# GpSimd computes no powers between the blocks of four transfers of its scatters

## The chip, the cores and the metric

One of the eight cores of a Trainium2 chip runs the whole kernel, in one launch. The metric is the time of one execution on the device, in microseconds (us). A time given for the kernel is the median of several executions.

## What is computed

The layer is a "macaron": feed-forward, attention, feed-forward, over 4096 tokens of 256 numbers.

```python
x = x + 0.5 * ffn(layernorm(x))
x = x + attn(layernorm(x))
x = x + 0.5 * ffn(layernorm(x))

def ffn(x):                                 # both times with the same weights
    tidx, tw = route(x)                     # 4 of 16 experts per token, and their weights
    routed = sum(tw[k] * mlp(x, expert[tidx[k]]) for k in range(4))
    return routed + mlp(x, shared)          # the shared expert is 2 x 128 wide
```

Each `mlp` is `silu(x @ gate.T) * (x @ up.T) @ down.T` with 128 inner channels for an expert. The attention stage is a state-space scan with a convolution and a gate; the change does not touch it. All of it is in fp32.

## The kernel before

**Tokens and blocks.** The 4096 tokens lie in SBUF as 32 blocks of 128 (`xn`, `xin`). They are routed in three groups g = 0, 1, 2 of 12, 12 and 8 blocks. Two neighbouring blocks or tiles form a pair, the unit of TensorE's work.

**Scatter.** Once VectorE has worked out where each token's four copies go (`rows`, line 719), GpSimd writes every block of `xn` four times to a table `xg` in HBM, sorted by expert: four indirect DMAs of 128 rows of 1 KB each (function `scatter`, line 426). A group's scatter starts when its `rows` are ready, and the groups come one after another. Before some blocks GpSimd computes a power of one element per partition into a tile `idle` that nobody reads (function `rest`, line 419). `REST_SCATTER` (line 38) says before which: 2 in group 0 (before blocks 2, 4, 6, 8 and 10), 1 in groups 1 and 2 (before every block but the first). During the scatter of group 0 GpSimd also computes the inverse standard deviations of the last four tiles of tokens, a power with a purpose (`rstd_of`, line 413): behind blocks 0 to 3 in the first stage, behind blocks 1, 2, 4 and 6 in the second.

**Experts.** SyncE loads four blocks of sorted rows at a time from `xg` into `xq` (line 335), the first ones when group 0 is scattered, the later ones when their group is. TensorE works through 78 pairs of sorted tiles. For each pair it turns the rows (`turn_x`, line 993, 4 matmul records), multiplies them by gate and up (`gate_up`, line 1025, 8 records), multiplies an earlier pair by down (`down`, line 1054, 4) and turns `h` of the pair before (`turn_h`, line 1038, 2): 18 matmul records in all. ScalarE copies the turned rows (`f_xT`, line 490), computes silu (line 503) and takes the output (`f_yo`, line 513); VectorE multiplies (line 768) and copies `h` turned (line 776). SyncE stores the output to `yg` (line 339).

**Order.** A written list of events sets what all engines do: while group 0 is being scattered, TensorE is on the router's products (line 1009) and the shared expert (lines 1030 and 1054); while group 1 is, on the last of these and the first pairs of group 0; while group 2 is, on further pairs of group 0. VectorE routes the next group meanwhile.

**Gather.** When enough pairs are stored, GpSimd fetches for each block four times 128 rows of `yg` into one of four buffers `gbuf` (function `gather_group`, line 452), and VectorE adds them up (line 791). A gather has no power between its blocks (`REST_GATHER` is zero); its first four blocks go out back to back, and later ones wait for VectorE to free a buffer.

Everything here happens in both feed-forward stages, the first at about 0 to 560 us, the second at about 1120 us to the end, apart from small differences in the order of the events.

Of the kernel before, what the change touches and what calls it, by code (L numbers as in the profile page):

```python
# [34 lines left out]
XQ = 4  # L35
YO = 4
GBUF = 4
REST_SCATTER = (2, 1, 1)
REST_GATHER = (0, 0, 0)
PIECES_W = [(0, SH), (SH, SH + 6), (SH + 6, SH + 11), (SH + 11, NU)]  # L40
FIRST_NORMALIZE = {("route", 5): 3, ("both", 6): 4, ("both", 8): 5, ("shared", 2): 6, ("shared", 3): 7}
# [101 lines left out]
def ffn_stage(nc, whole, consts, label, base, banks, src, dst, scratch, w, shared_sems, nth, spots=None):  # L143
# [250 lines left out]
    def gpsimd(pool, other):  # L394
# [22 lines left out]
        def rest():  # L417

            G.tensor_tensor(idle[:, rests[0]:rests[0] + 1], ones_m[:, 0:1], half_neg[:, 0:1], ALU.pow)
            rests[0] += 1  # L420

        def scatter(g, b):
            if REST_SCATTER[g] and b and b % REST_SCATTER[g] == 0:
                rest()
            for k in range(4):
                G.indirect_dma_start(xg[0:USED[g] * P, :], bass.IndirectOffsetOnAxis(ap=rows[g][:, b, k:k + 1], axis=0),  # L426
                                     xn[:, SUB * TILE0[g] + b, :], None, bounds_check=USED[g] * P - 1,
                                     oob_is_err=False).then_inc(scattered[g], 16)
# [1942 lines left out]
```

## Time and profile before

| | |
|---|---|
| median of three executions | 1679.23 us (1678.22 to 1689.73) |
| the profiled execution | 1694.23 us |
| its span, first to last instruction | 1692.4 us |
| its mean granted TensorE clock | 0.899 |
| GpSimd busy | 951.7 us (56%) |
| indirect DMAs of the scatters | 256 |
| indirect DMAs of the gathers | 256 |
| powers of line 419 | 46 |

The profiled execution's own time lies 1.83 us above its span. In the rows, PE is TensorE's matmuls, PEld its weight loads, DVE VectorE, ACT ScalarE, POOL GpSimd and SPq the queue of SyncE. Starts are counted from the first instruction. The ends of matmuls are modelled, so a matmul can have been finished later than its record says; a few per cent of the matmul records can be missing. "issue" is a wait for nothing that the profile shows, "remote" one that nothing in the profile of this core explains. An indirect DMA's record on POOL is the time in which GpSimd makes its descriptors, not the transfer.

### The profile page before, as it was taken

Reading aid. Unit: us, or ns where it says so; the run is one execution under the profiler, and the core shown is the slowest. Engines: PE = TensorE matmul, PEld = TensorE weight load, DVE = VectorE, ACT = ScalarE, POOL = GpSimd, SP = SyncE. Lnnn points to the kernel's source line nnn. Section 1 sums busy time; section 2 is a strip of 40 time slices with the busy share of each in tenths; the row PEclk is TensorE's granted clock in tenths of the full one; section 3 lists DMA queues with packets and bytes.
Section 4 is the critical chain, followed back from the end, with each engine's and each line's share of the span. In section 5 each row is a group of like instructions: output and inputs, shape, how many; then the busy total and the mean of one; then the engine's idle time right before and its main releaser. Section 6 shows DMA issues by size and latency. Waiting matters only on the chain.

```text
span 1692.4 us, 22687 instructions
## 1 busy us (share of the span) xinstructions
PE 1345.6 (80%) x6904; PEld 1143.0 (68%) x6904; DVE 905.1 (53%) x2190; ACT 658.4 (39%) x1088; POOL 951.7 (56%) x1002
## 2 busy tenths in 40 slices
PE   5847577968959969999999999969564599696890
PEld 5736465857847747888888887857554488585780
DVE  5626251224436798888888878765353122352453
ACT  2222232423424445656656665523311134242330
POOL 2664835054264668878878977417466701634535
PEclk9869788989989979999999999989687899798895
DMA  9951344546555520001000000234324435565633
GB/s 362 401 185 66 112 144 143 168 154 200 191 182 182 185 89 13 26 15 38 26 26 25 25 23 11 87 131 168 113 103 140 149 118 171 164 212 187 196 131 99
DMA packets 86917, 218.39 MB, mean 129 GB/s; under 512 B 16272, under 2 KB 28560, under 8 KB 85904
## 3 DMA queue, kind: packets, MB, share of 16 engines
q1 hardware_dynamic: 62224, 149.82, 25.1%
q0 software_dynamic: 24576, 67.14, 12.5%
q8 instruction: 58, 0.95, 0.2%
q14 instruction: 59, 0.48, 0.1%
HBM read 109.43 MB, written 107.48 MB: 128 GB/s over the span
## 4 chain that ended last, share of the span: by engine, by line
PE 54%; DVE 16%; issue 15%; another core or an unknown queue 9%; ACT 3%; POOL 2%; DVEq 0%; POOLq 0%; DMA 0%; ACTq 0%
PE ps L1025 14%; PE ps L1054 9%; PE ps L993 5%; PE ps L1030 5%; DVE at_xs L1784 3%; PE ps L1984 3%; PE ps L1986 3%; PE ps L1985 3%; PE ps L2045 2%; PE ps L1038 2%; DVE f_xin L791 2%; PE ps L1009 2%; PE ps L2046 1%; PE ps L2034 1%
## 5 line engine op out<-in xcount | busy, mean ns | idle before, releaser
L452 POOL DMA_INDIRECT f_gbuf<-yg,f_rows x256 | 263.0, 1027 | 389.8 <-DMA yg<-f_yo 243.7
L426 POOL DMA_INDIRECT xg<-f_xn,f_rows x256 | 253.8, 991 | 180.1 <-DVE f_rows L719 110.0
L1025 PE MATMUL ps<-f_wgu,f_xT 128*128 x1248 | 322.9, 405 | 17.9 <-issue 15.2
L1054 PE MATMUL ps<-f_wd,f_hT 128*128 x624 | 181.2, 417 | 144.2 <-issue 81.9
L1025 PEld LDWEIGHTS ps<-f_wgu,f_xT 128*128 128x128 f32 x1248 | 244.9, 207 | 53.1 <-issue 22.1
L768 DVE TENSOR_TENSOR f_h<-ps,f_sg 128x256 f32<-128x256 f32 x156 | 66.1, 424 | 377.8 <-ACT f_sg L503 242.1
L1054 PEld LDWEIGHTS ps<-f_wd,f_hT 128*128 128x128 f32 x624 | 124.3, 205 | 175.9 <-issue 159.1
L490 ACT COPY f_xT<-ps 128x512 f32<-128x512 f32 x212 | 124.2, 586 | 219.6 <-remote 100.0
L503 ACT ACTIVATE f_sg<-ps 128x256 f32<-128x256 f32 x156 | 60.1, 385 | 289.6 <-PE ps L1025 160.9
L1030 PE MATMUL ps<-f_xT,f_wgu_sh 128*128 128x256 f32 x512 | 135.2, 422 | 24.7 <-issue 12.0
L1784 DVE SCALAR_TENSOR_TENSOR at_xs<-at_raw,at_taps,at_xs 128x512 f32<-128x512 f32 x136 | 138.4, 1020 | 6.9 <-POOL at_xs L1435 4.2
L513 ACT COPY f_yo<-ps 128x512 f32<-128x512 f32 x156 | 91.5, 587 | 120.9 <-PE ps L1054 55.2
L1030 PEld LDWEIGHTS ps<-f_xT,f_wgu_sh 128*128 128x128 f32 x512 | 107.0, 215 | 43.7 <-issue 24.6
L791 DVE SCALAR_TENSOR_TENSOR f_xin<-f_gbuf,f_w,f_xin 128x256 f32<-128x256 f32 x256 | 128.3, 502 | 12.4 <-DMA f_gbuf<-yg,f_rows 5.4
L993 PE MATMUL ps<-ident,f_xq 128*128 128x128 f32 x624 | 105.9, 298 | 16.4 <-DVE f_counts L652 10.1
L776 DVE COPY f_hT<-ps 128x256 f32<-128x256 f32 x156 | 66.0, 423 | 95.9 <-remote 64.8
L2045 PE MATMUL ps<-at_wout,at_ynT_hi 128*128 128x256 f32 x512 | 98.0, 292 | 6.6 <-DVE at_ynT_lo L1793 5.2
L1434 POOL TENSOR_SCALAR at_tap<-at_raw,at_taps 128x512 f32<-128x512 f32 x56 | 93.2, 1665 | 5.6
L993 PEld LDWEIGHTS ps<-ident,f_xq 128*128 128x128 f32 x624 | 83.2, 155 | 18.5 <-issue 17.7
L2045 PEld LDWEIGHTS ps<-at_wout,at_ynT_hi 128*128 128x128 f32 x512 | 81.1, 195 | 12.7 <-DVE at_ynT_lo L1793 8.2
L1477 POOL TENSOR_TENSOR at_S_split<-at_S,at_S_split 64x1024 fp32r<-64x1024 f32 x31 | 74.2, 2394 | 10.5 <-ACT at_S_split L1670 10.3
L1435 POOL TENSOR_TENSOR at_xs<-at_xs,at_tap 128x512 f32<-128x512 f32 x56 | 75.8, 1354 | 4.7
(258 smaller groups left out, 2655.7 us busy)
## 6 DMA issues: line engine op xcount, KB each, us to landing
f_xq<-xg SPq DMA_DIRECT2D x78, 512.0 KB
yg<-f_yo SPq DMA_DIRECT2D x156, 256.0 KB
xg<-f_gbuf SPq DMA_DIRECT2D x39, 512.0 KB, 5.9
f_wgu<-in_gate_up SPq DMA_DIRECT2D x4, 1280.0 KB
f_xin<-in_x SPq DMA_DIRECT2D x8, 512.0 KB, 7.0
xg<-f_xn,f_rows POOLq DMA_INDIRECT x256
f_gbuf<-yg,f_rows POOLq DMA_INDIRECT x256
x<-f_xin SPq DMA_DIRECT2D x8, 512.0 KB, 4.1
```

The source lines that it names most:

```text
L426: G.indirect_dma_start(xg[0:USED[g] * P, :], bass.IndirectOffsetOnAxis(ap=rows[g][:, b, k:k + 1], axis=0), xn[:, SUB * TILE0[g] + b, :], N ...
L452: G.indirect_dma_start(gbuf[:, n % GBUF, k, :], None, yg[0:USED[g] * P, :], bass.IndirectOffsetOnAxis(ap=rows[g][:, b, k:k + 1], axis=0), ...
L490: A.copy(xT[:, k % 2], turned(k)).then_inc(xT_ready, 1)
L513: A.copy(yo[:, n % YO, :], y_ps[:, yy % 2]).then_inc(y_out, 1)
L791: ins = V.scalar_tensor_tensor(out=xin[:, n // SUB, n % SUB, :], in0=gbuf[:, n % GBUF, k, :], scalar=w4[g][:, b, k:k + 1], in1=xin[:, n // ...
L993: last = T.transpose(turned(k)[:, c:c + P], of[s][:, d * P:(d + 1) * P], ident[:])
L1025: last = T.matmul(gu_ps[:, j % 2, s * 2 * P:(s + 1) * 2 * P], x_of(k, s, d), weight(wgu[:, :, d, :], experts[s]), start=(d == 0), stop=(d ...
L1030: last = T.matmul(gu_ps[:, j % 2, half * 2 * P:(half + 1) * 2 * P], wgu_sh[:, experts[0], d, half * P:(half + 1) * P], xT[:, k % 2, 2 * d ...
L1054: last = T.matmul(y_ps[:, yy % 2, s * D:(s + 1) * D], hT[:, i % 4, s * P:(s + 1) * P], weight(wd if kind == "routed" else wd_sh, experts[i ...
L1434: link(G.tensor_scalar(tap0[:], raw[:, j % 2, 0:TILE], taps[:, j, 0:1], None, ALU.mult))
L1784: ins = V.scalar_tensor_tensor(out=acc, in0=raw[:, j % 2, k:k + TILE], scalar=taps[:, j, k:k + 1], in1=acc, op0=ALU.mult, op1=ALU.add)
L2045: nc.tensor.matmul(xu_ps[:, 0, 0:D], ynT_hi[:, j, :], wout[:, j, i, :], start=(j == 0 and i == 0), stop=False)
```

## The change

The constant that places the powers of the scatters is set to zero, so that `rest` is never called. Nothing else changes.

```diff
-REST_SCATTER = (2, 1, 1)
+REST_SCATTER = (0, 0, 0)
```

On POOL, group 0's scatter in the first feed-forward stage (`f_rows_150` holds the addresses of group 0, L413 are the inverse standard deviations; the piece begins behind block 2 of 0 to 11):

```order
 L413 TENSOR_TENSOR f_rstd<-f_var,f_half_neg 128x4
-L419 TENSOR_TENSOR f_idle<-ones,f_half_neg 128x1
-L426 DMA xg<-f_xn,f_rows_150 8192x256 x8
-L419 TENSOR_TENSOR f_idle<-ones,f_half_neg 128x1
-L426 DMA xg<-f_xn,f_rows_150 8192x256 x8
-L419 TENSOR_TENSOR f_idle<-ones,f_half_neg 128x1
-L426 DMA xg<-f_xn,f_rows_150 8192x256 x8
-L419 TENSOR_TENSOR f_idle<-ones,f_half_neg 128x1
-L426 DMA xg<-f_xn,f_rows_150 8192x256 x8
+L426 DMA xg<-f_xn,f_rows_150 8192x256 x32
 L1441 TENSOR_SCALAR at_rate<-at_rate 128x1
```

Four runs of eight DMAs become one run of 32.

On POOL, the end of group 2's scatter in the first stage and, in the rows with a plus, what stands for the whole scatters of groups 1 (`f_rows_151`) and 2 (`f_rows_152`):

```order
-L426 DMA xg<-f_xn,f_rows_152 19968x256 x4
-L419 TENSOR_TENSOR f_idle<-ones,f_half_neg 128x1
-L426 DMA xg<-f_xn,f_rows_152 19968x256 x4
+L426 DMA xg<-f_xn,f_rows_151 14336x256 x48
+L426 DMA xg<-f_xn,f_rows_152 19968x256 x32
 L452 DMA f_gbuf<-yg,f_rows_150 128x256 x48
```

Runs of four become one run of 48 and one of 32. Between these two, POOL still waits for group 2's rows.

On POOL, group 0's scatter in the second stage (`f_rows_272`), behind block 2:

```order
-L426 DMA xg<-f_xn,f_rows_272 8192x256 x4
-L419 TENSOR_TENSOR f_idle<-ones,f_half_neg 128x1
-L426 DMA xg<-f_xn,f_rows_272 8192x256 x4
-L413 TENSOR_TENSOR f_rstd<-f_var,f_half_neg 128x4
-L426 DMA xg<-f_xn,f_rows_272 8192x256 x4
-L419 TENSOR_TENSOR f_idle<-ones,f_half_neg 128x1
-L426 DMA xg<-f_xn,f_rows_272 8192x256 x4
-L413 TENSOR_TENSOR f_rstd<-f_var,f_half_neg 128x4
-L426 DMA xg<-f_xn,f_rows_272 8192x256 x4
-L419 TENSOR_TENSOR f_idle<-ones,f_half_neg 128x1
```

Here a power stood between any two of the blocks 1 to 8; what is left are runs of eight between the powers of line 413, and one run of 20 behind the last of them. The order on all other engines is the same, row for row.

## Rows read from the trace of the kernel before

**Rows 1.** The page: busy time, and the chain that ended last, by engine

```profile
PE 1345.6 (80%) x6904; PEld 1143.0 (68%) x6904; DVE 905.1 (53%) x2190; ACT 658.4 (39%) x1088; POOL 951.7 (56%) x1002
PE 54%; DVE 16%; issue 15%; another core or an unknown queue 9%; ACT 3%; POOL 2%; DVEq 0%; POOLq 0%; DMA 0%; ACTq 0%
```

**Rows 2.** Line 419 over the whole span: duration ns min/median/max

```profile
L419 POOL TENSOR_TENSOR f_idle<-ones,f_half_neg x46: 527/592/697, 62.7 to 1349.2; 128x1 f32<-128x1 f32 x46
```

**Rows 3.** Timeline of POOL, scatter of group 0, first stage: start, duration, idle before

```profile
85.57 0.97 POOL L426 DMA_INDIRECT xg<-f_xn,f_rows  x1 [0.31 <-issue]
86.85 0.97 POOL L426 DMA_INDIRECT xg<-f_xn,f_rows  x1 [0.30 <-issue]
87.83 0.58 POOL L419 TENSOR_TENSOR f_idle<-ones,f_half_neg 128x1 f32<-128x1 f32 x1
...
89.95 1.13 POOL L426 DMA_INDIRECT xg<-f_xn,f_rows  x1 [0.30 <-issue]
```

**Rows 4.** Timeline of POOL and SyncE's queue: who waits for a scatter's end

```profile
236.13 0.97 POOL L426 DMA_INDIRECT xg<-f_xn,f_rows  x1 [23.42 <-DVE f_rows L719]
348.48 1.05 POOL L452 DMA_INDIRECT f_gbuf<-yg,f_rows  x1 [68.03 <-DMA yg<-f_yo]
121.92 1.74 SPq L335 DMA_DIRECT2D f_xq<-xg  x4
```

**Rows 5.** Timeline of ACT and PE in group 1's scatter, first stage

```profile
185.75 0.60 PE L993 MATMUL ps<-ident,f_xq 128*128 128x128 f32 x4
194.38 0.59 ACT L490 COPY f_xT<-ps 128x512 f32<-128x512 f32 x1 [5.38 <-remote]
200.10 0.38 ACT L503 ACTIVATE f_sg<-ps 128x256 f32<-128x256 f32 x1 [5.13 <-PE ps L1025]
211.61 0.38 ACT L503 ACTIVATE f_sg<-ps 128x256 f32<-128x256 f32 x1 [5.87 <-remote]
```

**Rows 6.** Timeline of ACT in a gather of the first stage, without powers

```profile
355.71 0.59 ACT L513 COPY f_yo<-ps 128x512 f32<-128x512 f32 x1 [2.29 <-remote]
465.12 0.39 ACT L503 ACTIVATE f_sg<-ps 128x256 f32<-128x256 f32 x1 [3.04 <-remote]
482.20 0.39 ACT L503 ACTIVATE f_sg<-ps 128x256 f32<-128x256 f32 x1 [10.03 <-remote]
```

**Rows 7.** Windows: stretch, length, PE, PEld, DVE, ACT, POOL busy (count), clock, DMA share, GB/s

```profile
145.00:160.00 15.00, 14.19 (x57) 11.72 (x58) 8.20 (x28) 2.12 (x5) 11.96 (x13) 0.81 0.26 89
160.00:213.00 53.00, 28.13 (x111) 22.90 (x109) 13.61 (x44) 11.17 (x21) 42.45 (x47) 0.77 0.31 107
1232.00:1253.00 21.00, 16.88 (x74) 14.08 (x75) 15.03 (x57) 3.50 (x7) 16.41 (x18) 0.84 0.36 123
1253.00:1298.00 45.00, 19.34 (x66) 14.70 (x64) 5.70 (x34) 5.05 (x10) 36.12 (x41) 0.73 0.36 122
236.00:281.00 45.00, 28.67 (x110) 22.27 (x110) 9.99 (x34) 7.78 (x15) 35.61 (x39) 0.81 0.43 145
1311.00:1355.00 44.00, 24.46 (x105) 19.70 (x104) 9.02 (x30) 7.40 (x14) 35.18 (x39) 0.85 0.42 148
300.00:345.00 45.00, 45.00 (x251) 40.03 (x250) 11.89 (x28) 21.40 (x42) 0.00 (x0) 1.00 0.50 164
1150.00:1184.00 34.00, 30.70 (x166) 26.73 (x167) 18.20 (x56) 11.34 (x25) 23.75 (x26) 1.00 0.31 117
1184.00:1211.00 27.00, 12.92 (x78) 11.14 (x76) 10.23 (x54) 9.73 (x17) 20.59 (x22) 0.77 0.28 97
86.00:121.00 35.00, 15.15 (x56) 12.04 (x56) 5.38 (x18) 7.01 (x11) 27.14 (x29) 0.64 0.46 164
```

**Rows 8.** Windows as in rows 7: three gathers without powers, POOL back to back

```profile
356.00:380.00 24.00, 8.66 (x33) 6.42 (x32) 5.08 (x11) 2.44 (x5) 18.17 (x19) 0.70 0.46 143
466.00:484.00 18.00, 4.20 (x20) 2.86 (x19) 2.69 (x6) 1.56 (x3) 13.83 (x14) 0.84 0.52 162
1545.00:1571.00 26.00, 9.24 (x38) 6.83 (x37) 5.00 (x11) 2.73 (x5) 19.05 (x20) 0.79 0.46 141
```

## The prediction

> **What bounds the kernel now.** I read the page first. TensorE is busy for 80% of the span and carries 54% of the chain that ended last; GpSimd is busy for 56% and carries 2% [rows 1]. So GpSimd's time is not what the kernel waits for, and a shorter GpSimd program gains nothing by itself. The next view is the line of the powers: 46 of them, 592 ns each, 27 us of GpSimd's time [rows 2]. The timeline of GpSimd then shows what one costs in place: between the starts of the DMAs at 86.85 and 89.95 lie 3.10 us with a power, where two steps without one take 2 x 1.28 us (85.57 to 86.85) [rows 3]. That is 0.54 us; I use 0.55.
>
> Who waits for a scatter's end? Group 2's scatter starts when VectorE has its rows, after 23.42 us of idle time behind group 1's. The first gather starts after 68.03 us of idle time behind group 2's. SyncE loads the first sorted rows at 121.92, right behind group 0's scatter, but TensorE multiplies the first of them only at 178 us [rows 4]. Nobody stands and waits for the last scatter of a group.
>
> The last view is the one that matters, the windows by stretch [rows 7]. With GpSimd silent (300 to 345 us) TensorE issues 251 matmul records in 45 us, 5.6 per us. In the scatters it issues far fewer: 111 in 53 us, 66 in 45, 56 in 35. The timeline says how this looks: TensorE turned rows at 185.75, and ScalarE, idle, copies them only at 194.38, with a wait that the profile puts to "remote"; two silus are 11.5 us apart (200.10 to 211.61) [rows 5], where a pair of 18 records would take 18/5.6 = 3.2 us. So TensorE's results arrive late while GpSimd issues indirect DMAs, and TensorE, the bound, stands still for want of them. This is where the change acts.
>
> **Does a pause of GpSimd help TensorE?** Three things say so. First, stretches of the second stage: from 1150 to 1184 a power stands between any two blocks (some of them the longer ones of line 413, and one wait), and TensorE issues 166 records in 34 us, 4.9 per us; from 1184 to 1211 a power stands only after each second block, and it issues 78 in 27 us, 2.9 per us [rows 7]. Second, the start of a group: in group 1 the pace holds for some 15 us (57 records, 3.8 per us) and 21 us (74 records), and breaks down after that [rows 7]. In the gathers, which have no powers, the first late result comes soon: ScalarE was free for it at 355.71 - 2.29 = 353.4 and started at 355.7, which is 4.9 to 7.2 us behind the first DMA at 348.48; I use 5.4 [rows 4, 6]. Third, the level it falls to: in three gathers 33, 20 and 38 records in 24, 18 and 26 us, together 91/68 = 1.34 per us, with silus 17.1 us apart in the second [rows 6, 8]. With powers the scatters show 111/53 and 66/45, together 177/98 = 1.81 per us [rows 7].
>
> **The rule that speaks against this.** The rows show TensorE slowed while GpSimd issues indirect DMAs (rows 7, 66 records in 45 us against 251). The Trainium skill, "SBUF — State Buffer", section "Who interferes with whom", says that only the ports shared by VectorE and GpSimd cause contention and that TensorE has its own. By that rule the powers cost TensorE nothing and protect it from nothing, and the sum would be zero. The trace agrees that a DMA's record is not stretched, but TensorE's results do come late, so the rule is not the whole story here.
>
> **The change part by part.** Removed are 46 powers: 5 + 11 + 7 in each of two stages. Nothing is added; no DMA moves past another or past a wait. POOL's queue behind them (the next group's wait, the gathers) only comes earlier. For each scatter I count what TensorE gets done in it before and after. A scatter gets shorter by 0.55 us for each power. In it TensorE keeps its first pace for 5.4 us, then runs at S records per us, and what is left is done at 5.6 per us. S is the unknown: no scatter without powers is in the trace. Its nearest rows are the gathers without powers, so I take S = 1.35. Its ends are 1.81 (pauses do not matter to the level) and 1.0. The lower one is an estimate: a scatter's DMAs follow each other without the longer pauses that in [rows 7] go with 1.81, and the step from 1.81 to 1.34 is carried on by three quarters.
>
> - Group 1, first stage: 168 records in 68 us. After: 62 us, with 5.4 x 3.8 = 21 and 56.6 x 1.35 = 76, so 71 are left, 12.7 us. Sum 74.7, that is +6.7 us.
> - Group 1, second stage: 140 records in 66 us. After: 60 us, with 5.4 x 3.5 = 19 and 54.6 x 1.35 = 74; 47 left, 8.4 us: +2.4.
> - Group 2, first stage: 110 records in 45 us. After: 41.2 us, with 5.4 x 3.8 = 21 and 35.8 x 1.35 = 48; 41 left, 7.3 us: +3.5.
> - Group 2, second stage: 105 records in 44 us. After: 40.2 us, 21 and 47; 37 left, 6.6 us: +2.8.
> - Group 0, second stage: 244 records in 61 us. Four powers go, 58.8 us are left. The runs are now of eight with the power of line 413 between them, then one of 20. If the runs of eight hide as they did, only the last 20 us are slow: 20 x 1.35 + 38.8 x 4.9 = 217, 27 left, 4.8 us: +2.6. If the second half of each run of eight is slow too, 30 us are: 40 + 141, 63 left, 11.2 us: +9.0. I take the middle, +6.
> - Group 0, first stage, from 86 to 121: already slow, 56 records in 35 us. After: 33.4 us with 45; 11 left, 2 us: +0.4; the stretch before 86 loses one power, no change.
>
> The sum is 6.7 + 2.4 + 3.5 + 2.8 + 6 + 0.4 = 21.8, say +22 us. All these stretches lie one behind the other on TensorE, which sets the end, so they add. The gathers keep their order and cost nothing. With S = 1.0 the slow 240 us of these six (57 + 55 + 36 + 35 + 25 + 33) lose 240 x 0.35 / 5.6 = 15 us more, +37. With S = 1.81 they gain 240 x 0.46 / 5.6 = 20 us, which makes +2: the pause then helps only through the later onset.
>
> The profiled execution took 1694.23 us, 15 us above the median of the runs shown. Its time would become 1716; carried to the median of 1679.23 the forecast is 1701 us, with a range of its own of 1681 (S = 1.81) to 1716 (S = 1.0).
>
> **The rivals.**
>
> *A fixed share per DMA (faster).* Each indirect DMA might let a fixed number of TensorE's results through, pause or not. Then a power in a slow stretch only delays all, and its removal gives its full 0.55 us. 33 of the 46 powers lie in slow stretches (3, 9 and 5 in the groups of the first stage; 2, 8 and 6 in the second): 33 x 0.55 = 18 us, 1661 us. For it: ScalarE's steps of 5.7 us (194.38 to 200.10) [rows 5] look like four DMAs and their power. Against it: gathers without powers let fewer records through per DMA, 91/53 = 1.7 [rows 8] against 177/71 = 2.5 in group 1's scatters (88 operations of POOL less 17 powers) [rows 7], and the pace of 4.9 from 1150 to 1184. It decides if the records per DMA stay at 2.5.
>
> *The powers touch nothing.* The late results come with the scatter and would come as late without powers; the level differs in gathers for their own reasons (they write SBUF, scatters write HBM). What is saved on GpSimd is saved where nobody waits: 1679 us. This is also what the rule on the ports gives. For it: GpSimd's 2% of the chain. Against it: the difference between 4.9 and 2.9 records per us within one scatter.
>
> *Choked (slower still).* Without any pause TensorE's results might not get through at all behind the first 5.4 us: S = 0, and 240 x 1.35 / 5.6 = 58 us on top of the 22: 1759 us. Against it: the gathers still let 1.34 through [rows 8].
>
> **How the numbers follow.** The forecast has 0.60, the fixed share 0.13, no effect 0.20, choked 0.07. Run to run, about 1%, 17 us, can be told from no change. Of the forecast's 0.60, which spans 1681 to 1716, 0.50 lies above 1696, 0.08 within 1% and 0.02 below. Slower: 0.50 + 0.07 + 0.01 of the second rival = 0.58. Same: 0.08 + 0.17 + 0.02 of the first = 0.27. Faster: 0.11 + 0.02 + 0.02 = 0.15. The range runs from 1666, which leaves out most of the fixed share, to 1726, beyond S = 1.0 by another 10 us for a lower clock behind longer stalls: the clock was 0.64 to 0.85 in slow stretches and 1.00 in the free one [rows 7].
>
> **What would show it.** In the new profile: no row of line 419; POOL 46 x 0.55 = 25 us shorter in all its scatters; the first late result of ScalarE 5 to 6 us behind the start of groups 1 and 2, not 15 to 20; silus in group 1 some 13 to 18 us apart, not 11.5; 1.0 to 1.8 records per us in the slow part. It is wrong if group 1's scatter of 62 us holds 2 or more records per us of TensorE, or if the pairs done by its end are as many as before. It is half wrong if the level falls and the kernel is no slower, because something that I count as TensorE's work waits for VectorE anyway.

## The result, and the profile after

The changed kernel takes 1752.68 us (median of four executions, 1750.12 to 1754.06), the kernel before, run beside it, 1684.48 us (1678.22 to 1694.87). The ratio is 1.0453, with a 95% interval of 1.0401 to 1.0506: slower by 68 us. The forecast was 1701 us, with a range up to 1726. Here and below the ratio is estimated from undisturbed executions, so it need not be the quotient of the medians (1.0405 here); five executions of the experiments were left out of it as disturbed, among them three of the 26 of the kernel before on the first chip, A (1674.85, 1883.65 and 4528.40 us).

The profiled execution took 1754.06 us, its span is 1752.2 us against 1692.4. The page of the changed kernel, busy times and the chain that ended last, as [rows 1]:

```profile
PE 1340.0 (76%) x6904; PEld 1138.9 (65%) x6904; DVE 904.8 (52%) x2190; ACT 658.3 (38%) x1088; POOL 927.4 (53%) x956
PE 51%; issue 17%; DVE 16%; another core or an unknown queue 9%; ACT 3%; POOL 2%; DMA 1%; DVEq 0%; POOLq 0%; SPq 0%; ACTq 0%
```

GpSimd has 46 operations and 24.3 us less, as it should. No engine has more work; 60 us were added, and TensorE was busy in none of them (1340.0 us against 1345.6). The timeline of GpSimd shows where, in the starts of the scatters and gathers (as [rows 4]; start, duration, operation, idle time before it):

```profile
260.16 0.98 POOL L426 DMA_INDIRECT xg<-f_xn,f_rows  x1 [47.32 <-DVE f_rows L719]
...
381.27 1.05 POOL L452 DMA_INDIRECT f_gbuf<-yg,f_rows  x1 [80.31 <-DMA yg<-f_yo]
...
1270.58 0.97 POOL L426 DMA_INDIRECT xg<-f_xn,f_rows  x1 [25.95 <-DVE f_rows L719]
...
1360.32 0.97 POOL L426 DMA_INDIRECT xg<-f_xn,f_rows  x1 [28.50 <-DVE f_rows L719]
...
1492.14 1.06 POOL L452 DMA_INDIRECT f_gbuf<-yg,f_rows  x1 [91.12 <-DMA yg<-f_yo]
```

In the first stage, group 2's scatter starts at 260.16, before at 236.13, and the first gather at 381.27, before at 348.48 [rows 4]. GpSimd's wait for VectorE's rows ahead of group 2 doubled, from 23.42 to 47.32 us. Taken from start to start, so that each stretch is a scatter and the work behind it, the loss lies here:

| stretch, from a scatter's start to the next one's or the gather's | stage 1 | stage 2 |
|---|---|---|
| group 0 | +6.0 us | +3.6 us |
| group 1 | +18.0 us | +11.8 us |
| group 2 | +8.8 us | +9.9 us |

The six sum to 58.1 of the 59.8 us that the span grew by. The rest of the kernel, attention above all, lost 1.7 us.

The windows of the changed kernel (length, then busy time and records of PE, PEld, DVE, ACT, POOL, granted clock, DMA share, GB/s) answer [rows 7]:

```profile
151.00:167.00 16.00, 14.45 (x63) 12.02 (x64) 7.85 (x27) 1.74 (x4) 12.10 (x13) 0.90 0.27 92
167.00:213.00 46.00, 8.46 (x24) 5.80 (x22) 3.16 (x8) 0.97 (x2) 35.17 (x36) 0.58 0.30 103
213.00:260.00 47.00, 34.86 (x174) 30.13 (x174) 24.57 (x116) 19.82 (x38) 0.00 (x0) 0.83 0.26 86
266.00:301.00 35.00, 10.12 (x41) 7.53 (x39) 2.92 (x9) 1.99 (x5) 26.74 (x28) 0.65 0.36 124
1276.00:1332.00 56.00, 13.07 (x53) 10.32 (x52) 9.88 (x37) 1.94 (x4) 42.73 (x44) 0.63 0.35 117
1366.00:1401.00 35.00, 11.33 (x41) 8.51 (x39) 2.93 (x9) 1.94 (x4) 26.78 (x28) 0.65 0.37 124
```

In group 1's scatter TensorE keeps its pace for some 16 us (63 records) and then gets through 24 records in 46 us, 0.52 per us; with powers it was 111 in 53 [rows 7]. The other scatters give 41 in 35, 53 in 56 and 41 in 35. The granted clock falls to 0.58, next to the lower level of 1.2 GHz, behind an engine that does almost nothing.

The timeline of ScalarE in that stretch, as [rows 5], shows two silus 45 us apart (171.80 and 216.66), where the forecast had 13 to 18, and one copy between them:

```profile
164.79 0.38 ACT L506 ACTIVATE f_sg<-ps 128x256 f32<-128x256 f32 x1 [4.41 <-remote]
171.80 0.38 ACT L506 ACTIVATE f_sg<-ps 128x256 f32<-128x256 f32 x1 [6.63 <-remote]
197.06 0.59 ACT L490 COPY f_xT<-ps 128x512 f32<-128x512 f32 x1 [24.87 <-remote]
216.66 0.38 ACT L506 ACTIVATE f_sg<-ps 128x256 f32<-128x256 f32 x1 [19.01 <-remote]
```

What is held up is TensorE itself, not the news that it is done. The timeline of PE shows the four records that turn one pair's rows:

```profile
179.53 0.27 PE L993 MATMUL ps<-ident,f_xq 128*128 128x128 f32 x1 [0.48 <-issue]
182.32 0.37 PE L993 MATMUL ps<-ident,f_xq 128*128 128x128 f32 x1 [2.52 <-issue]
184.45 0.37 PE L993 MATMUL ps<-ident,f_xq 128*128 128x128 f32 x1 [1.76 <-issue]
187.25 0.37 PE L993 MATMUL ps<-ident,f_xq 128*128 128x128 f32 x1 [2.43 <-issue]
```

In the code no wait stands between these four, and in [rows 5] they are one unbroken run of 0.60 us. Here they start 2.1 to 2.8 us apart. VectorE, in the same microseconds, works at its full pace, a step each 0.4 us:

```profile
186.47 0.35 DVE L761 TENSOR_TENSOR f_tot<-f_sc,f_s 128x192 f32<-128x192 f32 x1
186.85 0.36 DVE L762 TENSOR_TENSOR f_tot<-f_tot,f_wt 128x192 f32<-128x192 f32 x1
187.25 0.35 DVE L763 TENSOR_REDUCE f_w<-f_tot 128x12 f32<-128x192 f32 x1
```

The last thing to see is what happens behind the scatter, in the timeline of VectorE. L612 begins the routing of group 2, whose last step, L719, releases its scatter. The kernel before:

```profile
193.86 0.28 DVE L612 TENSOR_TENSOR f_sc<-f_score,f_bias 128x128 f32<-128x128 f32 x1
...
235.16 0.19 DVE L719 TENSOR_TENSOR f_rows<-f_si 128x32 int32<-128x32 int32 x1
```

and the changed one:

```profile
217.15 0.42 DVE L772 TENSOR_TENSOR f_hT<-ps,f_sg 128x256 f32<-128x256 f32 x1 [28.37 <-ACT f_sg L506]
...
233.51 0.28 DVE L612 TENSOR_TENSOR f_sc<-f_score,f_bias 128x128 f32<-128x128 f32 x1
...
259.19 0.19 DVE L719 TENSOR_TENSOR f_rows<-f_si 128x32 int32<-128x32 int32 x1
```

Before, 19 of the 41 us that the routing took ran under group 1's scatter. Now VectorE stands for 28 us at a product of TensorE that is ahead of the routing in its order, and the whole of the routing, 25.7 us, comes behind the scatter.

What TensorE does between the scatter's end (212.83) and group 2's start (260.16) falls into three parts. Windows of the changed kernel, first of this stretch, then of the same one in the second stage (1331.83 to 1360.32):

```profile
213.00:222.30 9.30, 0.00 (x0) 0.00 (x0) 3.31 (x8) 3.79 (x7) 0.00 (x0) 0.50 0.04 14
222.30:230.00 7.70, 6.79 (x21) 5.63 (x22) 0.58 (x2) 3.77 (x8) 0.00 (x0) 0.55 0.00 0
230.00:260.00 30.00, 28.07 (x155) 24.49 (x153) 20.68 (x106) 12.26 (x24) 0.00 (x0) 1.00 0.39 130
1331.80:1336.90 5.10, 0.02 (x1) 0.03 (x1) 0.00 (x0) 0.59 (x1) 0.02 (x1) 0.50 0.07 26
1336.90:1342.00 5.10, 5.10 (x12) 4.07 (x13) 3.21 (x29) 1.74 (x4) 0.00 (x0) 0.50 0.15 53
1342.00:1360.30 18.30, 16.23 (x91) 13.98 (x89) 11.53 (x52) 7.79 (x15) 0.00 (x0) 1.00 0.45 156
```

First it does nothing, for 9.3 and 5.1 us. In the first stage the late result reaches ScalarE at 216.66, 3.8 us behind the scatter's last record, and TensorE's next product waits in the code for a tile that VectorE has finished only at 222.27:

```profile
222.11 0.16 DVE L1819 TENSOR_TENSOR at_flag_f<-at_flag_f 128x1 f32<-128x1 f32 x1
222.37 0.56 PE L2076 MATMUL ps<-at_flag_f,ones 128*128 128x1 f32 x2 [34.75 <-issue]
```

Then it works for 7.7 and 5.1 us at a granted clock of 0.55 and 0.50, the lower level, and gets through 21 and 12 records. Only then, at a clock of 1.00, does it catch up, at 155/30 = 5.2 and 91/18.3 = 5.0 records per us, and that with the routing beside it (233.51 to 259.38 in the first stage). The mean over the whole stretch is 174 records in 47 us, 3.7 per us.

### The profile page after: what moved, and what is told of

It reads as the page before. It is cut to its first block, busy times and chain, and to the rows that moved or that the text cites. A ratio compares the mean times of both kernels' runs of the same rounds, so it can differ in the third digit from the quotient of the medians.

```text
span 1752.2 us, 22641 instructions
## 1 busy us (share of the span) xinstructions
PE 1340.0 (76%) x6904; PEld 1138.9 (65%) x6904; DVE 904.8 (52%) x2190; ACT 658.3 (38%) x1088; POOL 927.4 (53%) x956
## 3 DMA queue, kind: packets, MB, share of 16 engines
q0 software_dynamic: 24576, 67.14, 12.0%
## 4 chain that ended last, share of the span: by engine, by line
PE 51%; issue 17%; DVE 16%; another core or an unknown queue 9%; ACT 3%; POOL 2%; DMA 1%; DVEq 0%; POOLq 0%; SPq 0%; ACTq 0%
PE ps L1025 14%; PE ps L1054 9%; PE ps L993 5%; PE ps L1030 5%; DVE at_xs L1784 3%; PE ps L1984 3%; PE ps L1986 3%; PE ps L1985 3%; PE ps L2045 2%; PE ps L1038 2%; DVE f_xin L791 2%; PE ps L1009 1%; PE ps L2046 1%; PE ps L2034 1%
## 5 line engine op out<-in xcount | busy, mean ns | idle before, releaser
L452 POOL DMA_INDIRECT f_gbuf<-yg,f_rows x256 | 267.5, 1045 | 412.9 <-DMA yg<-f_yo 268.6
L1025 PE MATMUL ps<-f_wgu,f_xT 128*128 x1248 | 326.8, 409 | 36.2 <-issue 20.6
L1054 PE MATMUL ps<-f_wd,f_hT 128*128 x624 | 176.8, 409 | 153.8 <-DVE f_hT L776 89.7
L772 DVE TENSOR_TENSOR f_hT<-ps,f_sg 128x256 f32<-128x256 f32 x64 | 26.2, 422 | 106.6 <-ACT f_sg L506 79.9
```

The lines of the kernel that those rows point to most:

```text
L452: G.indirect_dma_start(gbuf[:, n % GBUF, k, :], None, yg[0:USED[g] * P, :], bass.IndirectOffsetOnAxis(ap=rows[g][:, b, k:k + 1], axis=0), ...
L1025: last = T.matmul(gu_ps[:, j % 2, s * 2 * P:(s + 1) * 2 * P], x_of(k, s, d), weight(wgu[:, :, d, :], experts[s]), start=(d == 0), stop=(d ...
L1054: last = T.matmul(y_ps[:, yy % 2, s * D:(s + 1) * D], hT[:, i % 4, s * P:(s + 1) * P], weight(wd if kind == "routed" else wd_sh, experts[i ...
```

## The experiments

Eighteen runs, in five lots; the kernels of a lot share a chip. **The chips are not alike**, and the numbers can't be read without that. The kernel before takes 1441.5 us on the first (A), 1694.9 on B, 1671.6 and 1681.8 on C (two lots), 1677.9 on D. Every ratio is against the kernel before on the same chip.

| run | chip | median us | ratio, 95% interval |
|---|---|---|---|
| e1_g0off | A | 1436.87 | 0.9984, 0.9963 to 1.0004 |
| e2_g1off | A | 1440.75 | 1.0004, 0.9981 to 1.0027 |
| e3_g2off | A | 1440.57 | 1.0009, 0.9984 to 1.0034 |
| e4_double | A | 1448.01 | 1.0057, 1.0029 to 1.0085 |
| f1_changed | B | 1758.59 | 1.0395, 1.0339 to 1.0451 |
| f2_land | B | 1601.57 | 0.9439, 0.9403 to 0.9476 |
| f3_narrow | B | 1764.41 | 1.0396, 1.0340 to 1.0453 |
| f4_double | B | 1590.82 | 0.9358, 0.9306 to 0.9409 |
| h1_g1off | C | 1715.99 | 1.0234, 1.0168 to 1.0301 |
| h2_clump | C | 1696.37 | 1.0122, 1.0053 to 1.0190 |
| h3_both | C | 1537.25 | 0.9184, 0.9119 to 0.9250 |
| h4_triple | C | 1569.23 | 0.9380, 0.9319 to 0.9440 |
| j1_oob | C | 1738.46 | 1.0394, 1.0282 to 1.0507 |
| j2_g0off | C | 1693.42 | 1.0073, 1.0020 to 1.0126 |
| j3_g2off | C | 1702.54 | 1.0147, 1.0025 to 1.0269 |
| j4_both3 | C | 1558.83 | 0.9303, 0.9205 to 0.9401 |
| k1_gather2 | D | 1633.91 | 0.9746, 0.9696 to 0.9797 |
| k2_both | D | 1541.99 | 0.9205, 0.9161 to 0.9249 |

**A chip that shows none of it.** The first lot took the powers out of one group each, or doubled them all.

```diff
-REST_SCATTER = (2, 1, 1)
+REST_SCATTER = (0, 1, 1)     # e1; e2: (2, 0, 1); e3: (2, 1, 0)
```

```diff
-            G.tensor_tensor(idle[:, rests[0]:rests[0] + 1], ones_m[:, 0:1], half_neg[:, 0:1], ALU.pow)
-            rests[0] += 1
+            for _ in range(2):     # e4_double
+                G.tensor_tensor(idle[:, rests[0]:rests[0] + 1], ones_m[:, 0:1], half_neg[:, 0:1], ALU.pow)
+                rests[0] += 1
```

> The powers of group 0 alone are removed, those of groups 1 and 2 stay. Theory (each group's powers let TensorE's results through during that group's own scatter): the starts of the next stage of work in the two profiles put 6.0 + 3.6 = 10 us of the loss into group 0's scatters, so about 1694 us beside 1684, with the later groups' scatters as before. Rival (the loss sits in one queue that fills up over the whole stage, and group 0 fills it first): nearly the whole 68 us, 1740 or more. Rival (a fixed share per DMA): 5 x 2 x 0.55 us faster at most, 1679.

> The powers of group 1 alone are removed. Theory: the profiles put 18.0 + 11.8 = 30 us into group 1's scatters, so about 1714 us; TensorE's record count from 16 us behind the first DMA to the end of group 1's scatter in the first stage is near the changed kernel's 24, not the 111 of before. Rival (one queue over the whole stage): with group 0 and 2 still paused little happens, below 10 us.

> The powers of group 2 alone are removed. Theory: the profiles put 8.8 + 9.9 = 19 us into group 2's scatters, so about 1703 us; the three single removals add to about 60 to 68 us. Rival (a queue that needs more than 32 DMAs to fill): below 5 us.

> Two powers stand at each place where the kernel before has one, so GpSimd's scatters last 25 us longer in all. Theory (the pause is what lets TensorE's results through, and the kernel before still loses most of its pace: 111 records in 53 us against 5.6 per us): faster than before, by 20 to 60 us, 1625 to 1665; the first late result in group 1 comes later than 15 us or not at all. Rival (one power is enough, the rest of the loss is the scatter's own): 1684 plus 0 to 17 us, since the slow stretches get 25 us longer.

All four missed. No group's powers matter on this chip, and doubling them all costs 0.6%. Here group 1's scatter lies earlier, from 120.8 to 188.4 us in e1_g0off and from 122.9 to 185.3 in e2_g1off. A window inside it, first of e1_g0off, whose group 1 has its powers, then of e2_g1off, whose group 1 has none:

```profile
130.00:183.00 53.00, 45.52 (x232) 39.01 (x232) 32.95 (x141) 21.96 (x42) 42.68 (x48) 0.94 0.52 176
130.00:183.00 53.00, 45.68 (x232) 39.11 (x231) 32.66 (x141) 21.95 (x42) 40.58 (x41) 0.94 0.57 198
```

GpSimd does 48 operations in it with powers, where [rows 7] have 47, and TensorE issues 232 records where those rows show 111; without powers it issues 232 as well. The code of this scatter is the same and the pace of GpSimd is the same, so what the hold-up takes besides is a condition of the chip, or of the time at which this lot ran: chip A was met in one lot only (chip C was alike in two). Nothing here says which.

**The change again, and four kinds of pause or none.** The second lot met a chip like that of the result.

```diff
             if REST_SCATTER[g] and b and b % REST_SCATTER[g] == 0:
-                rest()
+                pool.wait_ge(scattered[g], 64 * (GB[g] * nth + b))     # f2_land
```

f1_changed is the changed kernel, f4_double is e4_double once more. f3_narrow is the changed kernel with 64 of each row's 256 numbers scattered, into a table of its own; the experts then work on rows of zeros, so its time is that of scatters with a quarter of the bytes.

> The changed kernel, word for word, measured again beside the kernel before. The last four runs were on a chip on which the kernel before takes 1441 us instead of 1684, and there no removal of a group's powers changed the time. Theory (TensorE's late results under indirect DMAs are a condition of the chip or its surroundings, and the powers only matter under it): where the kernel before takes 1684, the changed one takes about 1750; where it takes 1441, the changed one takes 1430 to 1445. Rival (three groups' powers together do what one alone does not): 1500 or more beside 1441.

> Each power is replaced by a wait until all earlier scatters of the group have landed, so GpSimd stands still for the landing time of a DMA, some 2 us, and computes nothing. Theory (what helps is that no indirect DMA is being issued or moved, not the power): where the kernel before takes 1684, at most 1684 and probably 1600 to 1650; where it takes 1441, 1445 to 1470, since the scatters get 60 us longer in all. Rival (the power itself matters): near the changed kernel, 1750, where the kernel before takes 1684.

> No powers; each scatter moves 64 of the 256 columns of a row, 256 bytes instead of 1 KB, into a table of its own that nobody reads, so the experts work on zero rows. The number of descriptors and GpSimd's time stay. Theory (it is the bytes in flight that hold TensorE up): where the kernel before takes 1684, the scatters show 4 or more matmul records per us and the time is 1600 or less. Rival (it is the descriptors, or GpSimd's making them): about 1750 there, with under 1.5 records per us. Where the kernel before takes 1441, both give 1430 to 1445.

> Two powers at each place, a second time. Theory: where the kernel before takes 1684, faster by 20 to 60 us; where it takes 1441, again about 8 us slower (1448), which is a third of the 25 us that GpSimd spends more, since there GpSimd's scatters are nearly the bound.

The change costs 64 us here, as in the result. Windows of the second part of group 1's scatter, f1_changed, then f3_narrow, f2_land and f4_double:

```profile
171.00:217.00 46.00, 10.42 (x28) 6.91 (x28) 3.16 (x8) 0.97 (x2) 34.63 (x36) 0.59 0.29 101
```

```profile
171.00:217.00 46.00, 9.82 (x26) 6.48 (x24) 3.18 (x8) 0.97 (x2) 34.64 (x36) 0.60 0.09 26
```

```profile
171.00:217.00 46.00, 39.66 (x201) 33.55 (x199) 24.90 (x113) 17.48 (x34) 23.42 (x24) 0.93 0.45 157
```

```profile
171.00:217.00 46.00, 41.77 (x210) 35.80 (x209) 28.35 (x132) 15.59 (x32) 37.74 (x45) 0.90 0.52 180
```

With a quarter of the bytes (26 GB/s against 101) TensorE does 26 records where it did 28: bytes are not it. A wait that computes nothing lets TensorE do 201 records, two powers 210, so it is not the power, it is that GpSimd makes no transfer for a while. f2_land pauses longer than it needs; its timeline of GpSimd:

```profile
175.04 0.98 POOL L426 DMA_INDIRECT xg<-f_xn,f_rows  x1 [4.06 <-DMA xg<-f_xn,f_rows]
176.33 0.98 POOL L426 DMA_INDIRECT xg<-f_xn,f_rows  x1 [0.31 <-issue]
```

And one power was too few: a second one in each place, 25 us more for GpSimd, takes 104 us off the kernel before, where I had expected 20 to 60. In f3_narrow it was the theory, bytes, that fell, and the rival that came true.

**Where the pauses stand, and how many.** h1_g1off is e2_g1off on chip C. h2_clump leaves group 0 alone and puts groups 1 and 2's powers three at a time, nearly the same number in all. h3_both doubles the powers and puts two before each gather block but the first; h4_triple has three powers at each place of the scatters, none in the gathers.

```diff
-            if REST_SCATTER[g] and b and b % REST_SCATTER[g] == 0:
+            for _ in range({3: 3, 6: 3, 9: 3}.get(b, 0) if g else (b in (2, 4, 6, 8, 10))):     # h2_clump
                 rest()
```

```diff
-REST_GATHER = (0, 0, 0)
+REST_GATHER = (1, 1, 1)     # h3_both, with rest() doubled as in e4_double
```

> The powers of group 1 alone are removed, a second time, in the hope of a chip on which the kernel before takes about 1684. There, theory (each group's powers protect TensorE during that group's own scatter): 30 us slower than the kernel before, as the two profiles have it (18.0 + 11.8), about 1.8%, with group 2's and 0's scatters as before. Rival (one queue that fills over the whole stage): under 10 us, or all 68. On a chip with 1441: no change, as in the first measurement.

> Groups 1 and 2 have their powers in heaps, three before each third block, so a run has 12 DMAs and a pause lasts 1.7 us; in all 9 powers instead of 11, and 6 instead of 7. Theory A (what counts is the sum of the pauses): where the kernel before takes 1684, 1680 to 1705. Theory B (the length of a run counts: TensorE is late from 5 to 8 us behind a pause, so short runs are needed): 1710 to 1740. Theory C (the first part of a pause is lost, long ones do more): below 1670. Where it takes 1441: no change.

> Two powers at each place of the scatters, and two before each block of a gather but the first. If pauses do for gathers what they do for scatters, then where the kernel before takes 1684 this gains more than the two powers of the scatters alone (94 to 104 us): the first four blocks of five of the six gathers cost TensorE about 17 us each in the old profile, half of that back is 40 us, so about 1550. Rival (gathers wait for free buffers anyway, and the last group's sit on the path to the end, 29 x 2 x 1.1 us of it): 1590 or more. Where it takes 1441: 1450 to 1470.

> Three powers at each place of the scatters. Where the kernel before takes 1684, two powers gave 1591 and TensorE issued 225 records in group 1's slow stretch against 111: 4.2 per us of 5.6. A third can give at most what is left, some 1.4 of 5.6 in about 200 us, 50 us, and costs 25 us of GpSimd's time, which is near the bound by then. Theory: 1570 to 1600, no clear gain over two. Where it takes 1441: about 16 us slower.

Group 1 alone costs 44 us, more than the 30 of the table above. Clumping costs 25 us (9 to 32 by the interval), which lies at the edge between theories A and B. It also has three powers fewer in each stage, 15 for 18 in groups 1 and 2. All 46 together are worth 64 to 68 us, so these six would be some 9 us, an estimate. What is left, some 16 us, says that a long pause each twelve transfers is worth less than short ones each four, but not by how much. h3_both is the fastest, 134 us below the kernel before; its window of group 1's scatter, to be set beside the 111 records of [rows 7]:

```profile
160.00:213.00 53.00, 46.48 (x247) 40.36 (x248) 30.19 (x137) 20.25 (x40) 43.52 (x51) 0.97 0.52 172
```

A third power adds nothing to the second in the scatters (0.938 on C, 0.936 for two on B).

**Making a transfer or moving rows.** j1_oob is the changed kernel with a bound that leaves nearly every row out.

```diff
-                                     xn[:, SUB * TILE0[g] + b, :], None, bounds_check=USED[g] * P - 1,
+                                     xn[:, SUB * TILE0[g] + b, :], None, bounds_check=0,
```

> The changed kernel, but each scatter's bound is 0, so nearly every row is out of bounds and is not moved; the experts then work on rows that are not the tokens', which is what is left out. GpSimd still issues every scatter. Theory A (what holds TensorE up is GpSimd's own work of making an indirect transfer, whatever is moved): on a chip on which the kernel before takes about 1680 us it stays near the changed kernel, 1740 to 1770 us, with fewer than 90 TensorE records between 160 and 213 us. Rival B (it is the DMA engines' moving of the rows): no hold-up without rows, TensorE keeps some 5 records per us there, and the time falls below the kernel before's, to 1640 us or less. On a chip on which the kernel before takes about 1441 us both expect 1430 to 1441 us and it tells nothing.

Its page shows the queue of GpSimd's transfers at 33.72 MB where the changed kernel has 67.14: the gathers' half is left, the scatters move nothing. Its queue row, and its windows:

```profile
q0 software_dynamic: 24576, 33.72, 7.2%
```

```profile
160.00:213.00 53.00, 10.18 (x45) 7.49 (x43) 4.01 (x10) 1.74 (x4) 38.18 (x40) 0.65 0.02 0
213.00:260.00 47.00, 36.68 (x182) 31.40 (x182) 26.16 (x123) 20.02 (x38) 2.03 (x3) 0.85 0.25 85
```

With the DMA engines at 2% and 0 GB/s TensorE does 45 records in 53 us, and 182 in 47 when GpSimd is done. The time, 1738 us, is a hair under the 1740 that I expected at least, and far from the rival's 1640. So the hold-up does not need the rows to be moved. What is left is GpSimd's own part, the making of descriptors, with what it writes and signals for them; those parts were not told apart.

**Does it add up?** j2_g0off and j3_g2off are e1 and e3 again.

> The powers left out of group 0's scatters alone (REST_SCATTER 0, 1, 1). In the changed kernel group 0 had 9.6 us of the loss. Theory A (the loss is made group by group and adds): on a chip on which the kernel before takes about 1680 us, +7 to +14 us. Rival B (group 0's two powers per place protect what follows): +20 us or more. On a chip with a before of about 1441 us: -1 to -5 us, as measured on such a chip.

> The powers left out of group 2's scatters alone (REST_SCATTER 2, 1, 0). In the changed kernel group 2 had 18.7 us of the loss. Theory A (adds group by group): +14 to +25 us on a chip on which the kernel before takes about 1680 us, and with group 1 alone (+44) and group 0 alone (+10) the three sum to 70 to 80 us, near the +68 of the whole change. Rival B (group 2 loses only because group 1's work runs late into it): +5 us or less. On a chip with a before of about 1441 us: within 2 us of it.

Alone, group 0 costs 12 us, group 1 44, group 2 21, together 77, against 64 and 68 for all at once. Each group's powers serve their own scatter, roughly: the intervals of the three are wide (3 to 21, 28 to 50 and 4 to 45 us).

**More pause, and the gathers.** j4_both3 is h3_both with three powers for two.

> Three powers at every place in the scatters and three before every gather block but the first. Three in the scatters beat one (0.938 of the kernel before) and stood beside two (0.936 on another chip); two in both gave 0.918. Theory A (two per place is enough, a third only adds GpSimd's time): 1535 to 1560 us on a chip on which the kernel before takes about 1680 us, not faster than two in both. Rival B (the more pause the better, TensorE is still held up in the gathers at two): below 1525 us. On a chip with a before of about 1441 us: 1455 to 1465 us, slower than before by the pauses alone.

0.930 against 0.918, on the same chip with the intervals touching: three are no better than two, which is all theory A needs.

k1_gather2 has the scatters as before, and two powers before each gather block but the first; k2_both is h3_both again.

> The scatters as before (one power at their places), and two powers before every gather block but the first. My forecast took the pace of TensorE without powers from the gathers, as if gathers and scatters hold it up alike. Theory A (they do, and a gather gains from pauses as a scatter does): on a chip on which the kernel before takes about 1680 us, 20 to 70 us faster, and more than 1.34 records per us in the gathers' busy stretches. Rival B (a gather does not gain, and h3_both was fast by its scatters alone): within 10 us of before, or slower. On a chip with a before of about 1441 us both expect up to 10 us slower.

> Two powers at every place of the scatters and two before each gather block but the first, once more, beside the kernel with the gathers' alone. Theory A: the two parts add; on a chip with a before of about 1680 us 1530 to 1565 us, 60 us or more below k1_gather2. Rival B (the gathers' powers give nothing): 1575 to 1600 us, as the scatters' two alone gave. On a chip with a before of about 1441 us: 1445 to 1460 us.

The gathers alone gain 44 us. What such a pause looks like in the timeline of GpSimd in k1_gather2, 1.10 us of power, and then two of the windows of [rows 8]:

```profile
346.67 1.10 POOL L420 TENSOR_TENSOR f_idle<-ones,f_half_neg 128x1 f32<-128x1 f32 x2
```

```profile
356.00:380.00 24.00, 21.48 (x109) 18.29 (x108) 12.96 (x30) 9.33 (x18) 19.84 (x24) 0.93 0.67 219
466.00:484.00 18.00, 14.74 (x66) 12.74 (x67) 10.14 (x24) 5.44 (x11) 14.75 (x18) 0.81 0.59 195
```

109 and 66 records stand where 33 and 20 stood, with GpSimd as busy as it was. Both parts together give 0.9205, so the scatters' second power gives the other 92 us.

## Why the prediction was right in sign and wrong in size

**What bounds the kernel, and that pauses help: right.** TensorE's results come late because GpSimd makes indirect transfers back to back, and pauses let it through. j1_oob, f2_land and k1_gather2 show it by experiment. "Nobody stands and waits for the last scatter of a group" held too: the first gather still comes 80.31 us behind it, when the tiles are stored.

**25 us off GpSimd, worth nothing: right** (24.3 us, 2% of the chain as before).

**The pace without powers, S = 1.35: wrong, between 0.5 and 1.2.** I took it from the gathers, which GpSimd issues at the same step. But their stretches in [rows 8] are 18 to 26 us long, with waits for VectorE's buffers around them, and a scatter's is 41 to 62 us without one; whether that or the scatter itself makes the difference was not tried. The lower end, 1.0, came from carrying one step on by three quarters; group 1 lies below it (24/46 = 0.52 and 53/56 = 0.95), group 2 between it and my value (41/35 = 1.17, twice). **The onset at 5.4 us: wrong the other way.** The first late result came at 164.79 after 4.41 us of idle time, that is 9.1 to 13.5 us behind the start at 151.24, and 63 records went through in 16 us. The two errors partly cancel. For groups 1 and 2 I had 97, 93, 69 and 68 records within the scatters, 327 in all. The windows from each start to each end have 86, 72, 56 and 56, 270. The 57 missing are 10 us at my 5.6 per us. Put into my own sum, these counts are S = 1.15, 0.97, 0.98 and 0.98 behind the first 5.4 us, close to its lower end, for which it gave 1716 us. So the pace within the scatters does not account for 1753.

**"What is left is done at 5.6 per us": wrong, the larger part of the error, and the step that failed.** The forecast has TensorE back at its free pace, that of 300 to 345 us [rows 7], the moment a scatter ends. The runs show it silent for another 9.5 us behind group 1's scatter in the first stage (212.83 to 222.37) and 5.1 in the second; behind group 2's it is 4.8 (300.96 to 305.71) and 4.9. Before, it was 2.4 behind group 1's in the first stage. Then come 5 to 8 us at the lower clock, and only then 5.0 to 5.6 records per us.

The sum with what was measured: in the first stage the stretch from the end of group 1's scatter to group 2's start grew from 23.4 to 47.3 us, by 23.9. It holds 166 - 86 = 80 records more, 14.3 us at 5.6 per us; the other 9.6 us are the rest, the slower restart above all. Less 5.9 us for the shorter scatter this is the +18.0, where I had 12.7 - 6 = +6.7. The other three go the same way, each number rounded by itself:

| | stretch behind the scatter | of it, records at 5.6 per us | of it, the rest | scatter shorter by | sum, measured | forecast |
|---|---|---|---|---|---|---|
| group 1, stage 1 | +23.9 us | 80: 14.3 us | 9.6 us | 5.9 us | +18.0 us | +6.7 us |
| group 1, stage 2 | +17.9 us | 66: 11.8 us | 6.1 us | 6.0 us | +11.8 us | +2.4 us |
| group 2, stage 1 | +12.3 us | 54: 9.6 us | 2.7 us | 3.5 us | +8.8 us | +3.5 us |
| group 2, stage 2 | +13.5 us | 49: 8.8 us | 4.7 us | 3.7 us | +9.9 us | +2.8 us |

The forecast had 12.7 + 8.4 + 7.3 + 6.6 = 35 us of catching up, and 68 were measured. Of the 33 us between them some 10 are the records missed within the scatters, and 23 are the rest, which the forecast put at nothing. The larger share of both is group 1's, +6.7 and +2.4 for what was +29.8.

The delayed routing looks like the cause of the slow catching up and is not. The mean pace behind group 1's scatter, 3.7 and 3.6 records per us, is that of no moment: with the routing beside it TensorE goes at 5.2 per us, and the silence and the lower clock come ahead of that.

**Group 0: +6.4 forecast, +9.6 measured**, but the other way about: first stage +0.4 against +6.0, second +6 against +3.6. The runs of eight between the powers of line 413 hid well (144 records in 36 us from 1171, 4.0 per us).

**The rivals.** *A fixed share per DMA* fell: 24 records in 36 operations of GpSimd, 0.7, where it wanted 2.5. *The powers touch nothing* fell on chips B and C and in the result and holds on chip A, where the whole effect is absent. The Trainium skill, "SBUF — State Buffer", section "Who interferes with whom", has it that "PE and ACT never wait on anyone". Chip A's rows agree (232 records in 53 us beside 48 operations of GpSimd, and 232 without powers); those of B do not (28 in 46 us without powers), and there the measurement decides. That it is a port at which TensorE waits there, no run shows. *Choked* had the size, 1759, but not its mechanism, which was luck: S was 0.5 to 1.2, not 0, and the rest came from the catch-up. I gave it 0.07 because the gathers let 1.34 through, and did not see that between S = 1.0 and S = 0 the catch-up could carry the time further than S itself.

**What stays open.** What in TensorE's path is stopped was not found. That the stop needs GpSimd's making of transfers and no bytes is shown, and that chip A had none of it; why it had none is not. The slow restart is read from the timelines, not shown by a run: why the last result comes some 4 us behind the scatter's last record, and what the silence and the lower clock would each cost alone, was not tried.

## What to carry to other kernels

Where GpSimd issues indirect DMAs beside a TensorE-bound stretch, look at matmul records per microsecond with GpSimd silent and with it busy. If they differ by several times, a pause of 1.1 us after each four transfers can be worth far more than it costs: 8% of this kernel, where the scatters' part of it cost 0.6% on the chip without the effect (the gathers' part was not run there). And price the end of a stall too: here TensorE had its first product only 5 to 9 us behind it and worked at the lower clock for 5 to 8 us more, so what a stall leaves undone costs more than its records at the best pace. Take one chip's time for no more than that chip's.

## What the runs showed that I had not expected

- One and the same kernel takes 1441 us on one chip and 1672 to 1695 us on three others, with 232 TensorE records in 53 us of group 1's scatter against 111 in [rows 7]. From 620 to 1000 us, in attention, where GpSimd issues no indirect DMA, the two sorts look alike: TensorE is busy for 358.6 of 380 us on chip A (e1_g0off) and for 364.7 in the kernel before.
- TensorE is held up with no bytes moving (0 GB/s, 45 records in 53 us), while VectorE in the same microseconds keeps its step of 0.4 us (j1_oob, steps at 177.58, 177.96 and 178.35).
- One power of 0.55 us per four transfers gives up most of the gain: 111 records in 53 us with one, 225 with two (f4_double, the same window), 227 with three (h4_triple). How much one power lets through differs too: the same window and group have 149 on chip D (k1_gather2) and 158 and 156 on C (j2_g0off, j3_g2off), group 1 as before in all three.
- The hold-up outlasts the scatter. In the changed kernel, behind the last record of each scatter of groups 1 and 2, the last late result of TensorE came after another 3.8 to 4.3 us, its next record after 4.8 to 9.5, and its granted clock was 0.50 to 0.58 in the first 5 to 8 us from there.
